# A graph-convolution kernel on one core: each 1152 KB unit of weights loaded as three 384 KB transfers, one behind the store of each of three consecutive steps

## The reference, cut to what matters

```
mean[n, r] = average of x[src] over the edges of relation r that end in n
conv(x)    = sum over r of mean[:, r] @ W[r]  +  x @ root  +  b
out        = layernorm(x + conv2(relu(conv1(x))))      # rows of 768, eps 1e-5
```

## Time and profile before

| | |
|---|---|
| median of three runs | 1479.65 us |
| the profiled execution | 1484.97 us |
| its span | 1483.2 us |
| mean granted TensorE clock | 0.996 |
| TensorE busy | 1461.7 us (99%) |
| VectorE busy | 991.3 us (67%) |
| ScalarE busy | 573.7 us (39%) |
| GpSimd busy | 576.7 us (39%) |
| DMA traffic | 249.72 MB, mean 168 GB/s |
| queue of GpSimd (q0) | 135.65 MB, 31.1% of 16 engines |
| queue of SyncE (q1) | 112.88 MB, 23.5% of 16 engines |
| loads of a unit | 35 of 1152 KB and 2 of 576 KB |

### The profile page before, as it was taken

How to read it: one execution, slowest core, us unless ns; L and a number is a source line. 1 busy time by engine, 2 the same in 40 slices (tenths; PEclk the granted TensorE clock), 3 DMA queues, 4 the chain that set the end, 5 groups by cost and what they waited for, 6 DMA issues and landing times.

```text
span 1483.2 us, 24220 instructions
## 1 busy us (share of the span) xinstructions
PE 1461.7 (99%) x9044; PEld 1448.4 (98%) x9044; DVE 991.3 (67%) x1594; ACT 573.7 (39%) x828; POOL 576.7 (39%) x458
## 2 busy tenths in 40 slices
PE   8999999999999999999999999999999999999998
PEld 8999999999999999999999999999999999999997
DVE  8899899957877677798651054545445354448887
ACT  4222211135444443466342333334333333317654
POOL 0000000056778874775306142424242424316553
PEclk9999999999999999999999999999999999999999
DMA  6453221268877786466328474646465655625454
GB/s 200 143 169 125 90 75 43 70 199 263 254 214 233 238 250 187 137 196 182 105 68 260 131 218 148 210 148 210 152 208 169 192 180 177 220 79 154 142 167 131
DMA packets 109596, 249.72 MB, mean 168 GB/s; under 512 B 20183, under 2 KB 83334, under 8 KB 109442
## 3 DMA queue, kind: packets, MB, share of 16 engines
q0 software_dynamic: 32480, 135.65, 31.1%
q1 hardware_dynamic: 77026, 112.88, 23.5%
HBM read 204.47 MB, written 65.49 MB: 182 GB/s over the span
## 4 chain that ended last, share of the span: by engine, by line
PE 87%; DVE 7%; issue 3%; DMA 1%; ACT 1%; SPq 0%; ACTq 0%; DVEq 0%
PE prod L841 67%; PE agg L887 15%; PE agg L841 2%; DVE slot_hot L1392 2%; PE prod L832 1%; DVE keyed L1400 1%; DVE dst_hot L1393 1%; PE agg L1007 1%; ACT g_high L696 1%; DMA x_rows<-in_x 1%; PE prod L887 1%; DVE key_hot L1385 1%; DMA raw<-y,bucket_index 1%; DVE g_low L1127 1%; DVE g_low L1131 0%
## 5 line engine op out<-in xcount | busy, mean ns | idle before, releaser
L841 PE MATMUL prod<-w_high,h_high 128*128 128x384 f32 x2100 | 709.0, 338 | 0.4 <-DVE acc L1105 0.4
L841 PE MATMUL prod<-w_low,h_high 128*128 128x384 f32 x2100 | 703.6, 335 | 0.0
L841 PE MATMUL prod<-w_high,h_low 128*128 128x384 f32 x2100 | 703.5, 335 | 0.0
L578 POOL DMA_INDIRECT raw<-y,bucket_index x346 | 454.5, 1314 | 513.4 <-DVE g_low L1131 250.6
L1131 DVE TENSOR_TENSOR g_low<-raw,g_high 128x768 fp32r<-128x768 f32 x246 | 225.6, 955 | 309.2 <-ACT g_high L696 265.6
L729 ACT ACTIVATE y_stage<-prod 128x384 f32<-128x384 f32 x280 | 137.9, 492 | 722.8 <-PE prod L841 591.8
L841 PEld LDWEIGHTS prod<-w_high,h_high 128*128 128x128 f32 x2100 | 395.5, 188 | 0.7 <-issue 0.7
L841 PEld LDWEIGHTS prod<-w_low,h_high 128*128 128x128 f32 x2100 | 395.7, 188 | 0.0
L841 PEld LDWEIGHTS prod<-w_high,h_low 128*128 128x128 f32 x2100 | 395.3, 188 | 0.0
L696 ACT ACTIVATE g_high<-raw 128x768 fp32r<-128x768 f32 x266 | 211.2, 838 | 64.6 <-PE agg L887 48.8
L887 PE MATMUL agg<-g_high,one_hot 128*128 128x384 f32 x720 | 188.8, 344 | 6.9 <-DVE g_low L1131 3.5
(11 more groups left out here) (161 smaller groups left out, 978.2 us busy)
## 6 DMA issues: line engine op xcount, KB each, us to landing
y<-y_stage SPq DMA_DIRECT2D x280, 168.0 KB
w_raw<-in_w_all SPq DMA_DIRECT2D x35, 1152.0 KB
raw<-y,bucket_index POOLq DMA_INDIRECT x346
y<-y_stage SPq DMA_DIRECT2D x280, 19.5 KB
y<-in_x SPq DMA_DIRECT2D x1, 3750.0 KB, 14.0
acc<-in_x POOLq DMA_DIRECT2D x10, 375.0 KB, 4.3
x_rows<-in_x SPq DMA_DIRECT2D x10, 336.0 KB
y<-acc SPq DMA_DIRECT2D x10, 336.0 KB
```

The costliest lines, as they stand in the source:

```text
L578: pool.indirect_dma_start(raw_rows(slot), None, y[0:written * N, :], bass.IndirectOffsetOnAxis(ap=bucket_index[:, at_column:at_column + 1] ...
L841: mm = pe.matmul(to, left[:, k, t * P:(t + 1) * P], right[:, h, k, :], start=(k == 0 and left is h_high and right is w_high), stop=(n == 0 ...
```

## The change

`load_unit` takes a range of pieces. Each piece is two of the six chunks, 384 KB, and raises `w_loaded` by 16; ScalarE waits for all three pieces of a unit. Only the first piece waits for `w_high_ready` and `w_low_ready` of the unit before. `load_pieces(q, s, at)` issues one piece at each of the steps at[h], at[h] + 1 and at[h] + 2, behind that step's store. Half 0 starts at step 8 in every matrix. Half 1 starts at step 14 in the table-free loops (q = 0 and q = 9 to 15), at 16 in q = 1 to 3 and at 17 in q = 4 to 6. The loads that stand outside the steps (unit 1 at the start, units 16 to 19 and the last two) are issued as three transfers in a row in their old places.

```diff
+    PIECES = 3
...
-            def load_unit(q, h):
+            def load_unit(q, h, pieces=range(PIECES)):
                 u = unit(q, h)
-                if not (isinstance(q, int) and u == 0):
+                if pieces.start == 0:
                     sp.wait_ge(w_high_ready, u)
                     sp.wait_ge(w_low_ready, u)
...
-                sp.dma_start(w_raw[:], w).then_inc(w_loaded, 16)
+                w = weights_of(q, h)
+                for n in pieces:
+                    k = slice(n * K // PIECES, (n + 1) * K // PIECES)
+                    sp.dma_start(w_raw[:, k], w[:, k]).then_inc(w_loaded, 16)
+
+            def load_pieces(q, s, at):
+                for h in range(2):
+                    if at[h] <= s < at[h] + PIECES:
+                        load_unit(q, h, range(s - at[h], s - at[h] + 1))
...
-            def relation(q, yc, r):
+            def relation(q, yc, r, at=(8, 14)):
                 for s in range(STEPS):
                     store_y(yc, r, s)
...
-                    if s == 8:
-                        load_unit(q + 1, 0)
-                    if s == 14:
-                        load_unit(q + 1, 1)
+                    load_pieces(q + 1, s, at)
...
             for q in range(1, ROOT1):
-                relation(q, q, q + 1)
+                relation(q, q, q + 1, (8, 17 if q >= TABLE_END else 16))
...
             def high_of_unit(q, h):
                 u = unit(q, h)
-                act.wait_ge(w_loaded, 16 * (u + 1))
+                act.wait_ge(w_loaded, 16 * (PIECES * u + 1))
```

More of the change, by code:

```diff
@@ L426, in banks, with weights_of @@
             return lambda s: 2 + s % 2 if turning and s >= T else (s + shift) % BANKS
+        def weights_of(q, h):
+            of = ([r - 1 + (r > R // 2) for r in range(1, R)] + [R // 2, R] +
+                  list(range(R + 2, 2 * R + 1)) + [R + 1, Q - 1])
+            m = of[q] if isinstance(q, int) else q + 1
+            return w_all[bass.ds(m, 1), :, h * HALF:(h + 1) * HALF].rearrange("o (k p) n -> p (o k) n", p=P)
         block = ctx.enter_context(nc.Block())
@@ L490, in _ @@
                 store_y(0, 1, s)
-                if s == 8:
-                    load_unit(1, 0)
+                load_pieces(1, s, (8, 14))
                 if s == 10:
@@ L499, in _ @@
                                  spilled_edges[:].rearrange("p c w -> p (c w)")).then_inc(table_cleared, 16)
-                if s == 14:
-                    load_unit(1, 1)
                 if s == STEPS - 1:
@@ L521, in _ @@
                 store_y(R - 1, 1, s)
[L522 to L525, removed]
+                load_pieces(MEAN1 + 2, s, (8, 14))
             with sp.Fori(2, R - 1) as r:
```

## The result

The changed kernel takes 1486.23 us (median of 5 runs, 1483.48 to 1489.81) against 1479.65 (5 runs, 1477.47 to 1479.85): ratio 1.0053, interval 1.0040 to 1.0066. The forecast was 1480.5 with 1475.5 to 1488. The full range held. The forecast's own range, 1477.5 to 1483, did not: the time lies between it and the rival that I had given 0.24, a new wait in the place of the old one with half clock behind it. (Half clock is a granted clock of 0.50, the 1.2 GHz level.)

What follows compares the result with a forecast made beforehand. The prediction took TensorE as the bound, busy 1461.7 of 1483.2 us. Its terms, -3.6 + 4.2 + 0.3 = +0.9 us, put on 1479.65 gave 1480.5 us, with a range of 1475.5 to 1488.

Steps and rivals of the forecast that it cites:

- The forecast's own range: Range of the case where gain and price cancel: 1477.5 to 1483 us around 1480.5, chance 0.36.
- the rival that I had given 0.24: ScalarE's copy behind step 11 of q = 4 to 6 waits for the last piece, two half clocks: +8.3, 1488.0 us; chance 0.24.
- half 1 of q = 4 to 6 moved: End of q = 5: SyncE no longer held with stores behind it, so ScalarE's wait for a store goes: -3.6 us, once.
- half 0 of q = 4 to 6: Last piece behind step 10 lands late for ScalarE's copy behind step 11, three times: +4.2 us.
- half 1 of q = 3: Last piece behind step 18 has 9.4 us before ScalarE wants it, first seven gathers between: +0.3 us, ends 0 and 1.0.
- loop: q = 10 to 15: half 0's last piece is late, but ScalarE's 2.11 us idle time covers it: 0, upper bound 4.2 us.
- cutting, 70 more issues: 70 more DMA issues on SyncE, 0.4 us of its queue each, fit into its waits: 0.
- the price: q = 4 to 6: half 0's last piece late for ScalarE's copy, passing 1:1 to TensorE, 1.4 us three times: +4.2 us.
- The bounds of the earlier trace: Limits for a last piece's landing after issue, q = 4 to 6: 3.5 us from below, 6.2 us from above.
- my signs of being wrong: ScalarE's copy never waiting for a DMA, half clock at three new places, or a loop period above 76.6 us.
- D: Lateness of half 0's last piece beyond its 3.6 us to land in q = 4 to 6: taken as 1.4 us, bounds 0 and 2.6.
- My third rival: End of q = 5: the 3.6 us wait is absent without a profile, the late pieces remain: 1484.2 us; chance 0.10.

Runs made afterwards that it cites:

- the kernel that has all units in place: Kernel before, with every unit sent as three 384 KB transfers in a row in its old place: 1477.76 us, ratio 0.9996.
- the price alone: Kernel before with half 0 of q = 4 to 6 behind steps 8, 9, 10; other units three transfers in a row, old places: 1482.52 us.
- the loop one step later: Old places for all units, but in q = 10 to 15 half 0 behind steps 9, 10, 11 and half 1 over 14, 15, 16: 1510.62 us.
- the two-sooner kernel: Changed kernel, but half 0 of q = 4 to 6 has its pieces behind steps 8, 9 and 9: 1480.91 us, ratio 1.0018.

## Why the prediction was right in its range and wrong in its likeliest time

Term by term, with differences of timed medians. The third column is against the kernel that has all units in place (1477.76 us, of another set for the first four rows), the fourth against the runs of before in the same set. They differ by up to 1.6 us, and neither is better than some 1.5 us:

| term | forecast | alone, against all in place | alone, against its own before |
|---|---|---|---|
| half 1 of q = 4 to 6 moved | -3.6 | -1.2 | -2.4 |
| half 0 of q = 4 to 6 | +4.2 | +4.8 | +3.2 |
| half 1 of q = 3 | +0.3 | +2.9 | +1.6 |
| loop | 0 | -0.4 | -1.7 |
| cutting, 70 more issues | 0 | | 0.0 |

**What held.** The place of the price (L688 behind step 11), its size (landing 5.3 us against 5.0, ScalarE waits of 0.94, 0.98 and 1.47 us), that it passes to TensorE, that the loop covers some 2 us of it (2.85 by the later test), and that the pause at the end of q = 5 came from SyncE's hold. The bounds of the earlier trace rows did their work: all three landings, 4.67 to 6.04 us, lie between 3.5 and 6.2, and one in the trace of the price alone, with 6.26 us, is just past them. Of my signs of being wrong one came in part: two of the six loop relations were longer than 76.6 us. The fit of a transfer in the Trainium skill (DMA: Bandwidth & Descriptors, "Anatomy of one DMA") gives 2.9 us for a piece; it was made with DMAs that GpSimd issues, and the pieces go through SyncE's queue. By it ScalarE would not have waited at all. The traces say 4.67 to 6.04 us beside gathers, so the measurement decides.

**That the range held is in part luck.** Its upper end, 1488.0, was three waits of D = 2.6 us and two half clocks behind them. The rival was to decide from D = 2.1 on; the trace has waits of 0.94, 0.98 and 1.47 us there and no half clock behind any of them. (Two later traces with the same places for half 0 each have one wait above 2 us with half clock behind it, so the rival's mechanism exists, but not three times over.) The time came near that end by other terms.

**The step that failed is the sum, in three terms.** First, "*Half 1 in q = 3* ... I take +0.3, with 0 and 1.0 as ends" was mis-sized: I gave the piece 9.4 us and asked only whether one gather would be ahead of it. It took 9.66. ScalarE's copy there already stood ahead of TensorE's pause: it began 0.81 us later than before (318.67 against 317.86), the bucket behind it 0.82 us later, and half clock followed. That makes 0.7 + 1.7 = 2.4 us in the trace, and 1.6 to 2.9 us by the timed runs. Second, "-3.6 us, once" was read from one execution with half clock in it. Without it that pause is 1.7 us, and the five other traces with the same hold have 0 to 1.35 us. The timed runs gained 0.7 to 2.4 us, by what they are held against. My third rival had said that the gain might not be in the timed runs; it was right in part. Third, half clock stood only in a rival, while the changed kernel makes three new pauses and one longer, and each of them can bring it.

**The clock goes with the spread.** The five timed runs of the changed kernel had mean granted clocks of 0.994 to 0.998, and their times follow: 1489.81 us at 0.994, 1486.23 at 0.996, 1483.48 at 0.998, so some 1.6 us for each 0.001. Against the 0.998 that is commonest for before, the 0.996 of the middle run would be some 3 of the 6.6 us: an estimate. Of the 87 runs of the kernel before in the first three sets, 31 had 0.999 with a median of 1476.6 us, 38 had 0.998 with 1479.0, and 17 had 0.997 with 1479.6, so the steps are not even.

**What stays open.** The single parts add up to 1477.76 - 1.2 + 4.8 + 2.9 - 0.4 = 1483.9 us, 2.4 less than the changed kernel's 1486.23; taken away from it, the two prices give 9.0, not 7.7. With the last column the parts add up to +0.7 us, or +2.4 without the loop, where the changed kernel has +6.6. So the single parts do not carry the whole. The loop's two late buckets (1.2 us in the trace) and further half clock are candidates, and neither was tested by itself. Also the pause of q = 6 was in none of the other traces at its place. ScalarE waited 6.77 us there to copy a product, with no releaser that names a cause, and 1.82 us of TensorE's idle time and half clock followed.

The version to keep is the one with the gain alone: half 1 of q = 4 to 6 behind steps 17 to 19 and everything else in place. Its 1476.60 us are the lowest median, 9.6 us below the changed kernel. Below before it is by 0.2% at most, and the single transfer behind step 17 (1477.02) can't be told from it.

## What to carry to other kernels

When a transfer is spread over steps, look at its last piece: it has the time from its own issue to the consumer, not that of the first. Where the consumer's engine is in series with the bottleneck without room (here a bucket that was already 0.2 us late behind ScalarE's copy), each us of it is a us of the kernel; one step sooner for the last piece took the price away (1480.91 us, as with the unit whole). And a change that frees a queue should be tried alone: moving the transfer took the pause away here, and the cut had no part in it that the runs could show.

## What the runs showed that I had not expected

A pause of the same length brings half clock in one execution and not in the next. In the table phase all these kernels have TensorE waiting about 2 us near 255. In the changed kernel the stretch behind it ran at a mean of 0.57:

```profile
258.00:262.00 4.00, 4.00 (x48) 4.00 (x46) 4.00 (x12) 0.00 (x0) 0.00 (x0) 0.57 0.01 4
```

In the two-sooner kernel, with the same pause, it ran at full clock:

```profile
258.00:262.00 4.00, 4.00 (x54) 4.00 (x52) 4.00 (x12) 0.00 (x0) 0.00 (x0) 1.00 0.02 4
```

0.57 over 4 us is 3.4 us at 0.50, worth 1.7 us of work. The pause near 255, of about 2 us, was followed by half clock in nine of the fourteen traces of this study. So such a pause is a lottery of some 1.7 us, by this estimate, and in the mean over runs it is worth more than its length. Other pauses: those of 1.69 and 1.82 us in the trace of before were followed by half clock, one of 1.5 us (q = 5 of the changed kernel with half 1 of q = 3 undone) was not, and those of about 3 us in the loop one step later were, in all six relations.
